# Selective scan with gates and a routed feed-forward layer on one core: another order of tasks, gates in four bursts, five places for weights

## What is computed

```
u   = silu(causal_conv4(ctx @ in_proj_w.T) + conv_b)          # (b, 1024 channels, l)
low, Bm, Cm = split(x_proj_w @ u, [32, 16, 16])
dt  = softplus(dt_proj_w @ low + dt_proj_b)
state = state * exp(dt * A) + (dt * u) * Bm                   # scan over l, 16 states
y   = sum over states(state * Cm) + D * u
x   = x + tanh(g_xattn) * y * silu(layernorm(x))
xf  = layernorm(x)
S   = softmax(xf @ router_w + router_b);  G, idx = top_k(S.T, 256)
x   = x + tanh(g_ffn) * scatter_add(idx, G * (xf[idx] @ expert_w + expert_b))
```

## Time and profile before

| | |
|---|---|
| median of three runs | 2237.96 us (2236.62 to 2238.84) |
| profiled execution, its time | 2250.82 us |
| profiled execution, its span | 2249.0 us |
| before the first scan | 66 us |
| halves 0 to 7, from first scan to first scan | 259, 242, 236, 240, 240, 243, 230, 216 us |
| after the last scan, until the search of the top 256 | 116 us |
| search and output | 160 us |
| PE, DVE, ACT, POOL busy | 74%, 86%, 61%, 76% of the span |

### The profile page before, as it was taken

One profiled execution on the slowest core, in us unless ns is written; L12 is line 12 of the kernel. 1 busy time (PEld: TensorE's weight loads), 2 busy tenths in 40 slices (PEclk: granted clock), 3 DMA queues, 4 the chain that ended last, 5 costly groups with the idle time before them and its releaser, 6 DMA issues.

```text
span 2249.0 us, 23467 instructions
## 1 busy us (share of the span) xinstructions
PE 1668.7 (74%) x7564; PEld 1064.5 (47%) x7564; DVE 1936.2 (86%) x2081; ACT 1371.7 (61%) x2326; POOL 1711.8 (76%) x606
## 2 busy tenths in 40 slices
PE   7467676678887888778887888787878787788720
PEld 2235445445554555445554555454555565544310
DVE  7989999988999899988997999889997899910587
ACT  3545766675778676766787676757786767622000
POOL 0578999987899899988998899878998999920000
PEclk9677788889898999999998999899998899999865
DMA  9500141134735383527443563337343734376078
GB/s 370 220 15 29 63 174 66 38 108 147 265 111 169 99 301 113 179 67 279 139 160 96 192 226 119 126 126 270 118 150 100 277 109 136 99 239 231 0 300 353
DMA packets 144219, 358.69 MB, mean 159 GB/s; under 512 B 15586, under 2 KB 18146, under 8 KB 134882
## 3 DMA queue, kind: packets, MB, share of 16 engines
q1 hardware_dynamic: 140354, 343.57, 43.1%
q10 hardware_dynamic: 3744, 13.63, 1.5%
HBM read 310.48 MB, written 46.66 MB: 159 GB/s over the span
## 4 chain that ended last, share of the span: by engine, by line
DVE 25%; PE 23%; issue 16%; POOL 13%; ACT 11%; DMA 9%; SPq 1%; ACTq 1%; DVEq 0%; POOLq 0%
DVE states L1002 15%; POOL states L1248 8%; PE pM L647 7%; PE pY L586 5%; PE pA L554 4%; POOL states L1236 4%; DMA sz<-in_x 4%; DMA wk<-in_expert_w 3%; DVE states L989 3%; ACT pDec L794 3%; DVE u L979 2%; PE pA L563 2%; ACT L936 2%; ACT sz L868 2%; DMA bbc<-x_scratch 1%
## 5 line engine op out<-in xcount | busy, mean ns | idle before, releaser
L1248 POOL TENSOR_TENSOR states<-states,cbc 128x2048 f32<-128x2048 f32 x256 | 1158.3, 4532 | 114.2 <-ACT carry L778 83.0
L794 ACT ACTIVATE pDec<-steps,an 128x512 f32<-128x512 f32 x1024 | 691.7, 687 | 441.9 <-DVE states L1002 439.6
L586 PE MATMUL pY<-con,states 128*128 128x128 f32 x4096 | 578.6, 303 | 144.3 <-POOL states L1248 144.1
L1002 DVE TENSOR_TENSOR_SCAN states<-pDec,carry,states 128x512 f32<-128x512 f32 x512 | 625.2, 1265 | 57.2 <-ACT pDec L794 57.0
L586 PEld LDWEIGHTS pY<-con,states 128*128 128x128 f32 x4096 | 532.9, 158 | 272.0 <-POOL states L1248 220.6
L1002 DVE TENSOR_TENSOR_SCAN states<-pDec,states 128x512 f32<-128x512 f32 x512 | 594.7, 1205 | 66.2 <-ACT pDec L794 65.7
L647 PE MATMUL pM<-wk,xfT 128*128 128x512 f32 x896 | 473.0, 634 | 78.7 <-DMA wk<-in_expert_w 75.4
L1236 POOL TENSOR_TENSOR states<-dtu,bbc 128x1024 f32<-128x1024 f32 x192 | 454.2, 2366 | 98.9 <-PE pY L586 81.4
L989 DVE TENSOR_TENSOR states<-pU,bbc 128x1024 f32<-128x1024 f32 x320 | 385.3, 1204 | 17.3 <-PE pY L586 14.0
L554 PE MATMUL pA<-ctx_sb,win 128*128 128x512 f32 x448 | 233.8, 671 | 53.3 <-issue 32.5
L647 PEld LDWEIGHTS pM<-wk,xfT 128*128 128x128 f32 x896 | 154.3, 202 | 173.3 <-issue 96.3
(11 more groups left out here) (174 smaller groups left out, 1394.9 us busy)
## 6 DMA issues: line engine op xcount, KB each, us to landing
wk<-in_expert_w SPq DMA_DIRECT2D x448, 256.0 KB, 4.2
bbc<-bc_scratch SPq DMA_DIRECT2D x32, 1024.0 KB, 6.5
cbc<-bc_scratch SPq DMA_DIRECT2D x32, 1024.0 KB, 9.0
sz<-in_x SPq DMA_DIRECT2D x16, 1024.0 KB, 7.4
xt<-in_x SPq DMA_DIRECT2D x15, 1024.0 KB, 5.6
win<-in_winT SPq DMA_DIRECT2D x58, 256.0 KB, 2.7
x_scratch<-xt SPq DMA_DIRECT2D x14, 1024.0 KB, 6.9
xr<-x_scratch SPq DMA_DIRECT2D x28, 512.0 KB, 4.2
```

What stands on the lines that cost most here:

```text
L586: mm = pe.matmul(pY[:, eT(t)], states[g % NST][:, i, eT(t)], ident, start=False, stop=(q == QG - 1 and i == QN - 1 and t == TT - 1), is_tr ...
L794: nc.scalar.activation(pDec[bank_of(h, k)][:], dt[e % 2], ACT.Exp, scale=an[:, k:k + 1]).then_inc(s_dec, 1)
L1002: nc.vector.tensor_tensor_scan(st, pDec[bank_of(h, k)][:], st, 0.0 if h % HB == 0 else carry[:, e, k % NS:k % NS + 1], ALU.mult, ALU.add). ...
L1248: nc.gpsimd.tensor_tensor(st, st, cbc[:, QW * q:QW * (q + 1), :], ALU.mult).then_inc(s_hc, 1)
```

## The change

- The bursts of ACT come after `late` in a slot instead of before it.
- `silu_u` goes from slot 44 to 42, the x projection from 46 and 47 to 44 and 45, `low` from 50 to 48, the add of the halo stays in 40. The first two input projections go from 51 and 55 to 49 and 54.
- sz is two places of two tiles: `load_gate` moves two tiles (512 KB) in slots 44 (of the half before), 2, 18 and 34, and `gate_silu` works on two tiles in slots 5, 13, 29 and 45. The seventh gate is turned in slot 48, not 50.
- `norm_x2` comes one slot later, `unit_out` one earlier. Product steps stand in slots 0, 1, 1, 2, 3, 3, 4, 5 of their unit, not 0 to 6 with two in the last. wk has five places, and a load stands three slots ahead of its step, not two.
- `load_dtp` stands 15 slots ahead of its dtproj, not 17.
- mhalf, a constant, is one column, and its wide form for the first layernorm lies in a scratch tile.

```diff
-IN_SLOT = [-77, -73] + [GQ * j - 85 for j in range(2, E)]
+IN_SLOT = [-79, -74] + [GQ * j - 85 for j in range(2, E)]
-HALO_SLOT, SILU_SLOT = [-24], [-20]
-XP_SLOT, LOW_SLOT = [-18, -18, -17, -17], [-14]
+HALO_SLOT, SILU_SLOT = [-24], [-22]
+XP_SLOT, LOW_SLOT = [-20, -20, -19, -19], [-16]
-SZ_SLOT = [5, 37]
-SZT_SLOT = [GQ * e + 9 for e in range(5)] + [43, 50, 65]
+SZ_SLOT = [5, 13, 29, 45]
+SZT_SLOT = [GQ * e + 9 for e in range(5)] + [43, 48, 65]
-XF_SLOT = [s + 4 for s in LN2_SLOT]
+XF_SLOT = [s + 5 for s in LN2_SLOT]
-STEP_SLOT = [s + min(k, E - 2) for s in UNIT_SLOT for k in range(E)]
-UO_SLOT = [s + 8 for s in UNIT_SLOT]
+STEP_SLOT = [s + k for s in UNIT_SLOT for k in (0, 1, 1, 2, 3, 3, 4, 5)]
+UO_SLOT = [s + 7 for s in UNIT_SLOT]
-NRING, NPIECE = 4, 3
+NRING, NPIECE = 5, 3
...
-                wait(sp, s_szp, n(h, E, part * (E // 2)))
+                wait(sp, s_szp, n(h, E, 2 * (part - 1)) if h or part else 0)
...
-                    :, part * (E // 2):(part + 1) * (E // 2), h % HB * T:(h % HB + 1) * T]
-                sp.dma_start(sz[:], src).then_inc(s_zx, 16)
+                    :, 2 * part:2 * (part + 1), h % HB * T:(h % HB + 1) * T]
+                place = part % 2 * 2
+                sp.dma_start(sz[:, place:place + 2, :], src).then_inc(s_zx[part % 2], 16)
...
-            GATE_SLOT = [2, 34]
+            GATE_SLOT = [44 - G, 2, 18, 34]
-            WK_SLOT = [s - 2 for s in STEP_SLOT]
+            WK_SLOT = [s - 3 for s in STEP_SLOT]
-            DTW_SLOT = [DTP_SLOT[e] - 17 for e in range(E)]
+            DTW_SLOT = [DTP_SLOT[e] - 15 for e in range(E)]
...
             def gate_silu(h, part):
-                wait(act, s_zx, n(h, 32, 16 * (part + 1)))
+                wait(act, s_zx[part % 2], n(h, 32, 16 * (part // 2 + 1)))
                 act.wait_ge(s_ln1b, 2 if h >= HB else 1)
-                for i in range(E // 2):
-                    e = part * (E // 2) + i
-                    nc.scalar.activation(sz[:, i, :], sz[:, i, :], ACT.Silu, bias=ln1[:, h // HB, 1, e:e + 1],
+                for e in range(2 * part, 2 * part + 2):
+                    gate = sz[:, e % (E // 2), :]
+                    nc.scalar.activation(gate, gate, ACT.Silu, bias=ln1[:, h // HB, 1, e:e + 1],
...
                     for e, k in at(DCP_SLOT, g, h):
                         dtu_copy(k, e)
+                    late(h, g)
                     steps_due = at(SP_SLOT, g, h)
...
                     if steps_due or silus or gates:
                         nc.scalar.preload_act_table_set(EXP)
-                    late(h, g)
```

More of the change, by code:

```diff
@@ L158, in mamba_moe @@
         ddiag = sb("ddiag", [P, P])
-        mhalf = sb("mhalf", [P, B, E])
+        mhalf = sb("mhalf", [P, 1])
         ctx_sb = sb("ctx_sb", [P, KC, T])
@@ L182, in mamba_moe @@
         mv1 = szT[0][:, 160:160 + 2 * NC * TT].rearrange("p (b e s) -> p b e s", b=B, e=E)
+        mhalves = szT[0][:, 280:280 + NC * TT].rearrange("p (b e) -> p b e", b=B)
         coef = szT[1][:, 0:TT * NC].rearrange("p (t c) -> p t c", t=TT)
@@ L264, in mamba_moe @@
         s_rs1 = sem("ln1_rstd")
-        s_zx = sem("gate_in")
+        s_zx = [sem("gates0_in"), sem("gates1_in")]
         s_bn = sem("ln2_steps")
@@ L443, in side @@
                     load_dtp(k, i)
+                if h == 0 and g == 2:
+                    load_gate(0, 0)
                 for i, k in at(GATE_SLOT, g, h):
@@ L497, in _ @@
             load_dtp(0, 2)
-            load_dtp(0, 3)
             for h in range(NC):
@@ L1109, in _ @@
             nc.vector.memset(one[:], 1.0)
-            nc.vector.memset(mhalf[:], -0.5).then_inc(s_c, 1)
+            nc.vector.memset(mhalf[:], -0.5)
+            nc.vector.memset(mhalves, -0.5).then_inc(s_c, 1)
             dve.wait_ge(s_w, 16 * NW)
@@ L1264, in rstd2 @@
                 wait(pool, s_bn, n(h, 3 * TT, 3 * t + 3))
-                nc.gpsimd.tensor_tensor(rs2[:, t:t + 1], ve2[:, t:t + 1], mhalf[:, 0, 0:1], ALU.pow).then_inc(s_pr, 1)
+                nc.gpsimd.tensor_tensor(rs2[:, t:t + 1], ve2[:, t:t + 1], mhalf[:], ALU.pow).then_inc(s_pr, 1)
                 pool.wait_ge(s_pr, n(h, TT, t + 1))
@@ L1291, in ln1_rstd @@
                 pool.wait_ge(s_ln1v, k)
-                nc.gpsimd.tensor_tensor(ln1[:, rows, 0, :], ve1[:, rows, :], mhalf[:, rows, :], ALU.pow).then_inc(s_rs1, 1)
+                nc.gpsimd.tensor_tensor(ln1[:, rows, 0, :], ve1[:, rows, :], mhalves[:, rows, :], ALU.pow).then_inc(s_rs1, 1)
             ln1_rstd(slice(0, 1), 1)
```

## The result

| us | before | changed |
|---|---|---|
| median of four runs | 2237.29 (2234.88 to 2238.84) | 2207.27 (2204.61 to 2209.31) |
| profiled span, first profile | 2249.0 | 2202.8 |
| profiled span, a second one | 2241.3 | 2206.3 |
| first scan to last scan, first and second profile | 1906.3, 1900.2 | 1874.0, 1876.2 |
| last scan to the first matmul of the search | 120.1, 118.6 | 105.9, 107.9 |

The changed kernel takes 0.9863 [0.9847, 0.9879] of the time before: 30 us faster, where 52 were forecast. The first profile of before was a long execution; a second one was 8 us shorter: 4 us in waits of DVE in slots 43 to 59, 2 in half 0 and 1.5 after the last scan. The 116 us that the prediction has for the stretch after the last scan end a few us earlier than the row here, at PE's products in front of the search; to that mark it is 116.6 and 115.1 us before, 102.4 and 104.3 now.

What follows compares the result with a forecast made beforehand. DVE was taken as busiest, its idle time left to win, with POOL a floor close beneath. Gates -25, end -20, norm_x2 -3, tail -10 made -58; 6 given back, -52: median 2238 to 2186 us, 8 in 10 for 2160 to 2224.

Steps and rivals of the forecast that it cites:

- the likeliest case: The forecast itself, 2186 us, given a chance of 0.65 and a range of its own from 2165 to 2207 us.
- the end of a half: Slots 43 to 59: -20 us, with the silu's +27 us within it; bounds +27 and -45.
- Gates, -25 us: Gate bursts of two tiles: each new one makes DVE wait 0.54 us, no load is waited for; between 0 and -35.
- The silu, 5.4 us: Silu in slot 42: DVE waits 5.4 us where it cost 1.53, POOL's addition just holds; +27 us in seven halves.
- What that buys, 64 instead of 84.1 us: DVE's waits in slots 43 to 59 of seven halves fall to 64 us, as PE gets the logits' copy earlier.
- The bound of -45 us: Best end for slots 43 to 59: PE's lateness ends as well, and 5.4 + 0.5 are left of 12 us.
- the rival that the end gains nothing: The silu's +27 us stays and PE is as late as before: 2227 us, chance 0.15.
- norm_x2, -3 us: One slot later, DVE's 1.13 us wait behind POOL's reciprocal root in slot 22 goes in three even halves; 0 otherwise.
- Tail, -10 us: After the last scan: five places 5 us, first pieces ahead of the whole matrix 2, clock 3; between 0 and -14.
- PE's waits for pieces in the halves, counted at nothing: PE's 65.5 us of waits in 60 places go, but lie beside DVE's work, so no gain was counted.
- Give back, +6 us: POOL waits longer for a saved carry at the silu, and part comes back as DVE waiting for sums: 6 us.
- Slower, bursts one by one: Rival, chance 0.07: each of 31 gate bursts costs DVE 1.9 us and the silu's +27 us stays; 2275 us.

Runs made afterwards that it cites:

- br_gates: Gates and product side changed as in the changed kernel, the end of the half as before; 2201.67 us, 0.9791 of the time before.
- a_split: The changed kernel with the silu in two bursts, blocks 0 to 5 in slot 36 and 6 and 7 in slot 43; 2194.79 us, 0.9761 of before.
- b_ring: The kernel before with the product side alone changed (steps, unit_out, norm_x2, five places, earlier loads, dtproj weight); 2221.27 us, 0.9906 of before.
- a_dtp17: The changed kernel with the dtproj weights loaded 17 slots ahead again; 2208.47 us, 0.9837 of before.
- a_silu43: The changed kernel with the silu of the next half in slot 43 instead of 42; 2208.28 us, 0.9818 of before.

## Why the prediction was right and where not

The time lay in the range (2160 to 2224), 21 us above the forecast of 2186 and just above the top of the likeliest case's own range (2207). That it lies in the wide range is partly luck: the end of a half, worth 20 us in the sum, gave next to nothing, and half 7 none of its 3, while the 6 us given back were not needed.

- **Gates, -25 us.** The price of a burst, 0.54 us, was measured at 0.41 to 0.59; without half 7 the waits at these slots fell by 22.1 us, as forecast. Half 7 was to give 3 us and gave none (idle 10.1 to 10.9 us): POOL's 213 us of work are its length, so the waits of 6.7 us at its old bursts came back at slots 3, 19, 46 and 50. The first load of a half stands 25 slots ahead of its burst and not "10 or 11", which changes nothing.
- **The silu, 5.4 us.** It was 5.1 in odd halves and 5.5 in half 0. In even ones it was 6.4, since "just holds" of POOL's addition did not hold (halves 4 and 6) and ACT stood for a gate in half 2. That is 3 us.
- **What that buys, 64 instead of 84.1 us.** This is the step that failed: it was 78.0, and with half 7 about 1 us was gained. (The bound of -45 us is 42.7 by its own figures, 6.1 us in seven halves.) Slots 46 and 50 (0.4 to 0.6, 1.5 to 1.7) and the end of the wait at slot 58 came as worked out. The term that was mis-sized most is slot 48: 19.6 us instead of six times 1.9 = 11.4. The arithmetic took PE's work behind the logits at the full clock, 1.9 us for two steps, though the earlier trace rows showed a projection at the lower clock after a wait of 3.24 us and PE was to wait about 4 us here. Half 0 had 9.4 us instead of 6. For this term the rival that the end gains nothing came nearer, and `br_gates` confirms that; the forecast's other terms held. Its reason, the silu ahead of the logits' copy on ACT, is only a part: in the even halves of `a_split` PE waits about 1 us for that copy and DVE 3.9 us at slot 48 all the same, because both x projections stand in front of the unit's last step. What the forecast did not see is whose gain this was. Its arithmetic had the unit's steps and `unit_out` in their new places as well, and the product side, to which they belong, brings the 20 us alone (`b_ring`, 62.4 us against 84 and 80); the moved x projections, silu and input projections take some back (`br_gates` is 5 us faster without them).
- **norm_x2, -3 us.** Slot 23 went from 3.4 to 0.
- **Tail, -10 us.** It was -14.2 between the first profiles and -10.7 between the second ones. The size was right. The reason, that the fifth place brings half of it, was too large: 1 to 5 us.
- **PE's waits for pieces in the halves, counted at nothing.** DVE did not gain them one by one, and no run shows that it gained anything from them: slot 49's 17 us in `b_ring` come with the steps' places, as shown above. SP's wait at the dtproj weight was to be gone and is still 247.4 us; `a_dtp17` has 710.4 us of it at no cost: with each load a slot earlier it keeps hardly a piece.
- **Give back, +6 us.** No such wait of DVE for sums was found; they fell by 15 us. POOL's share rose only to 78%.
- **The sum.** In the first profiles it is -46.2 us against -52 forecast, in the second -35.0, in the runs -30 and, beside the last group, -39. The forecast carried the waits of one long execution over to the median in full, and took off only its excess of 12.9 us from the total; 4 of the 8 us that the second profile lacked were in slots 43 to 59, where gains had been counted. The rest of the spread of before, 2235 to 2257, is open.
- **Slower, bursts one by one.** Excluded by 0.41 to 0.59 for each. The Trainium skill, ScalarE: Activation LUTs, section What ACT_TABLE_LOAD costs, with its drain of about 1380 ns for each switch, would have put a two-tile burst near 7 us (two switches and 1.52 us of silu), an estimate from that page; this trace has 4.13 us from 1189.96 to the next decay at 1194.09. The 32 further loads cost DVE no more than the 0.41 to 0.59 us at each burst, and two more loads in each half, of the split silu, came with a gain.

## What to carry to other kernels

Where a consumer has a short queue (here three decays), a burst on the producer costs its length less what is queued, so cut long bursts and put them where the producer is ahead; moving one without cutting it gave all of it back a few slots later (`a_silu43`). Look at which matmuls stand in front of the last one that a copy waits for: two large projections in front of a unit's last steps cost a wait at slot 48 in every half with products, at either clock, and the same projections behind them next to none. Price the work behind a wait of some microseconds on TensorE at both clocks, since the same place took 1.8 us or 4.1. Do not add the gains of parts that end at the same wait, and take the waits that you mean to remove from more than one profile.
